# Score and row-maximum matmuls of the softmax heads, divided over four 32-column tiles

## The chip, the cores and the metric

One core of a Trainium2 chip runs the whole program in one launch. The metric is device time in microseconds. Three runs of the kernel before gave 8461.63, 8458.88 and 8468.84 us, median 8461.63.

## The reference

The input is 4 images of 48 x 48 tokens (N = 2304) with 192 channels, and the program is a chain of residual blocks on it: rotary attention, a Fourier mixer, wide attention, a switch of experts, retention with a decay mask, and a projection by signs. The change touches the first block alone. There every image has 8 heads of width 12, so 32 heads in all, and what is computed for a head is

```
attn = einsum('bhnd,bhmd->bhnm', q * hd ** -0.5, k)      # 2304 x 2304
attn = softmax(attn, axis=-1)
out  = einsum('bhnm,bhmd->bhnd', attn, v)                # 2304 x 12
```

## The kernel before

The attention of the first block is the function `softmax_heads`. An earlier stage has split q and k of every head into three bf16 terms each, whose sum is the fp32 value. Stacked along the contraction they give products of terms: 8 x 12 = 96 rows. So every score is one bf16 matmul with 96 rows, or 99 where three further rows carry the negated row maximum in three bf16 terms against ones.

For each head the stage does two things. The **row maximum** goes through TensorE once: for each of 18 tiles of 128 queries (stationary, `q_next`), `max_chunk` (L522 to L535) multiplies by 5 chunks of keys (moving, `k_next`): four of 512 columns and one of 256, 90 chunks a head. A chunk is written to one of two PSUM buffers, `ring`; VectorE reduces it to a column (L624) and frees it by the semaphore `ring_free`, for which TensorE waits at L533 before chunk m+2. At the head's end VectorE reduces the 90 columns (L628), TensorE transposes them (L540), and VectorE splits them into terms (L632 to L641), which go through DRAM into the rows of q.

Then come 54 **steps**, one for each third of the queries (768) and each tile of 128 keys. `score` (L542 to L556) has the 128 keys stationary (`k_piece`) and the queries moving in two halves of 384 columns, into one of two PSUM buffers `scores`. ScalarE takes the exponential of the 768 columns (L664) into one of four buffers `probs`. `value` (L558 to L568) multiplies them by the values, fp32: the stationary operand is `v_piece`, 32 columns wide (12 values, a column of ones, zeros), and the 768 queries are divided into four groups of 192 moving columns, each of which is written to its own quarter of PSUM's partitions, so to its own 32-column tile of the array. The profile shows an fp32 matmul as two instructions with a load each, eight in a step.

The order of TensorE's work is written out in `exponentials` (L570 to L602): in step n the scores of n, then chunks, the values of n - 2, then chunks. The chunks belong to the next head; of its 90 chunks 23 (`AHEAD`) are done a head before that, the others are spread evenly by the list in `maxima`. A head thus has 108 places for 90 chunks, five in each six. The steps of two heads are written out in one body of a hardware loop, which runs 15 times; heads 30 and 31 follow it, with 67 chunks in head 30 and none in head 31. Before the loop the 90 chunks of head 0 run alone.

SyncE loads q, k and v of the next head, GpSimd loads `q_next` and `k_next` and stores the results; both wait on the same semaphores (`scored`, `valued`, `ring_full`), which the last matmul of a piece of work raises.

Of the kernel before, what the change touches and what calls it, by code (L numbers as in the profile page):

```python
# [8 lines left out]
P = 128  # L9
# [360 lines left out]
def softmax_heads(nc, q_parts, k_parts, q_runs, k_runs, v_rows, ident, m_rows, out_rows, N, d, scale):  # L370
# [16 lines left out]
    QC = THIRD // 2  # L387
# [4 lines left out]
    PT = TILES // PIECES  # L392
# [8 lines left out]
    with ExitStack() as ctx:  # L401
        sb, ps, sem = allocators(nc, ctx, "softmax")
        q_third = [sb(f"q_third{i}", [K + 3, THIRD], BF16) for i in range(3)]
        k_piece = [sb(f"k_piece{i}", [K + 3, PT * P], BF16) for i in range(PIECES)]
        v_piece = [sb(f"v_piece{i}", [P, PT, 32], F32) for i in range(PIECES)]
        q_next = [sb(f"q_next{i}", [K, N], BF16) for i in range(2)]
        k_next = [sb(f"k_next{i}", [K, N], BF16) for i in range(2)]
# [8 lines left out]
        scores = [ps(f"scores{i}", [P, 2, 512], F32) for i in range(2)]  # L416
        sums = [ps(f"sums{i}", [P, 512], F32) for i in range(2)]
        ring = [ps(f"ring{i}", [P, 512], F32) for i in range(2)]
# [5 lines left out]
        ring_full, ring_free = sem("ring_full"), sem("ring_free")  # L424
# [98 lines left out]
        @block.tensor  # L523
        def _(pe):
            def max_chunk(h, i, m):

                j, c = divmod(m, NC)
                at, width = CHUNKS[c]
                if m == 0:

                    pe.wait_ge(next_in[i], (h - i + 2) * 16 * RUNS)

                pe.wait_ge(ring_free, h * RING + max(m - 1, 0))  # L533
                return nc.tensor.matmul(ring[m % 2][:, 0:width], q_next[i][:, j * P:(j + 1) * P],  # L534
                                        k_next[i][:, at:at + width], start=True, stop=True).then_inc(ring_full, 1)  # L535

            def max_transpose(h):
                pe.wait_ge(ring_free, h * RING + MAXES - 1)
                pe.wait_ge(row_ready, h + 1)
                nc.tensor.transpose(ring[MAXES % 2][0:TILES, 0:P], row_max[:, :], identity[:, :]).then_inc(ring_full, 1)  # L540

            def score(h, n, first=False):  # L542
                third, t = divmod(n, TILES)
                if t == 0:
                    pe.wait_ge(q_in[third], (h + 1) * 16 * RUNS)
                    pe.wait_ge(maxes_in[third], (h + 1) * 16)
                if third == 0 and t % PT == 0:
                    pe.wait_ge(kv_in[t // PT], (h + 1) * 16 * (RUNS + 1))

                if n or not first:  # L550
                    pe.wait_ge(exped, h * STEPS + n - 1)
                for c in range(2):
                    last = nc.tensor.matmul(scores[n % 2][:, c, 0:QC],  # L553
                                            k_piece[t // PT][:, t % PT * P:(t % PT + 1) * P],
                                            q_third[third][:, c * QC:(c + 1) * QC], start=True, stop=True)
                last.then_inc(scored, 1)  # L556

            def value(h, n):  # L558
                third, t = divmod(n, TILES)
                pe.wait_ge(exped, h * STEPS + n + 1)  # L560
                if t == 0:

                    pe.wait_ge(copied, h * 3 + max(third - 1, 0))
                for g in range(4):
                    last = nc.tensor.matmul(sums[third % 2][32 * g:32 * g + 32, 0:VC], v_piece[t // PT][:, t % PT, :],  # L565
                                            probs[n % 4][:, g * VC:(g + 1) * VC],
                                            start=(t == 0), stop=(t == TILES - 1))
                last.then_inc(valued, 1)  # L568

            def exponentials(h, i, following):  # L570

                done = 0

                def maxima(n):

                    nonlocal done
                    turn, steps = 2 * TURN, 2 * STEPS
                    share = AHEAD + (MAXES - AHEAD) * (n + 1) // turn if n < turn else MAXES + AHEAD * (n + 1 - turn) // (steps - turn)
                    while following and done < min(share, MAXES if following == 1 else MAXES + AHEAD):
                        if done == MAXES:  # L580
                            max_transpose(h + 1)
                        if done < MAXES:
                            max_chunk(h + 1, 1 - i, done)
                        else:
                            max_chunk(h + 2, i, done - MAXES)
                        done += 1
                    if following == 1 and done == MAXES and n == turn:
                        max_transpose(h + 1)

                done = AHEAD  # L590
                for n in range(STEPS):

                    if n:
                        score(h, n)
                    maxima(2 * n)
                    if n >= 2:
                        value(h, n - 2)
                    maxima(2 * n + 1)
                if following:
                    score(h + 1, 0)  # L600
                value(h, STEPS - 2)
                value(h, STEPS - 1)  # L602

            pe.wait_ge(ident_in, 16)
            pe.wait_ge(ones_set, PIECES)
            for m in range(MAXES):
                max_chunk(0, 0, m)
            max_transpose(0)
            for m in range(AHEAD):
                max_chunk(1, 1, m)  # L610
            score(0, 0, first=True)
            with pe.Fori(0, n_heads // 2 - 1) as pair:
                for i in range(2):
                    exponentials(pair * 2 + i, i, 2)
            exponentials(n_heads - 2, 0, 1)
            exponentials(n_heads - 1, 1, 0)
# [2319 lines left out]
```

## Time and profile before

| | |
|---|---|
| median of 3 runs | 8461.63 us |
| span of the profiled execution | 8460.6 us |
| TensorE busy, of the span | 7417.9 us (88%) |
| weight loads busy | 3625.5 us (43%) |
| VectorE busy | 4769.0 us (56%) |
| ScalarE busy | 3185.4 us (38%) |
| GpSimd busy | 2338.1 us (28%) |
| the stage `softmax_heads` | about 297 to 2630 us |
| mean granted TensorE clock | 0.915 |

The profiled execution has no time of its own beside its span, from its first to its last instruction. PE is TensorE's matmuls, PEld its weight loads, DVE is VectorE, ACT is ScalarE, SP is SyncE. The time of a matmul is from its start to its modelled end; since the next one starts as soon as the columns of this one have streamed in, the difference of two starts says what a matmul costs, and its duration how long its result takes.

### The profile page before, as it was taken

What the parts mean: (1) busy time and instruction counts of PE and PEld (TensorE: products, weight loads), DVE (VectorE), ACT (ScalarE), POOL (GpSimd) and SP (SyncE); (2) the same over time, 40 slices, a digit from 0 to 9 for tenths busy, and PEclk for the clock granted to TensorE, in tenths of its full rate; (3) what the DMA queues carried; (4) which work ended last, traced back from release to release, by engine and by line L of the source; (5) the groups of instructions that cost most, each with busy time, mean ns of one, the idle gap of its engine ahead of it and who ended that gap; (6) DMA issues with size and microseconds to landing.
All of it is one profiled execution on the core that took longest, in us unless ns stands there. A gap on an engine that the chain in (4) does not pass through costs nothing. (4 is left out here: it accounts for less than half of the span.)

```text
span 8460.6 us, 164061 instructions
## 1 busy us (share of the span) xinstructions
PE 7417.9 (88%) x53035; PEld 3625.5 (43%) x53035; DVE 4769.0 (56%) x7714; ACT 3185.4 (38%) x5336; POOL 2338.1 (28%) x2558
## 2 busy tenths in 40 slices
PE   6799999999996775799999970997799999999987
PEld 4233333333333552576666760775433333333326
DVE  6777777777772401232232243114677777777766
ACT  2166666666663241222222210212444444444432
POOL 0011111111111000000000003002388888888861
PEclk8699999999998786899999965998899999999986
DMA  4211111111114314000000031114611111111113
GB/s 118 58 33 33 33 33 33 33 33 33 33 29 95 104 46 132 27 13 13 26 1 17 1 119 54 52 49 135 200 31 30 30 31 29 30 30 31 30 50 105
DMA packets 414311, 426.01 MB, mean 50 GB/s; under 512 B 76199, under 2 KB 386635, under 8 KB 408590
## 3 DMA queue, kind: packets, MB, share of 16 engines
q1 hardware_dynamic: 331790, 339.52, 14.2%
q0 software_dynamic: 62400, 59.16, 2.8%
q10 hardware_dynamic: 19712, 21.53, 0.8%
q8 instruction: 299, 4.90, 0.3%
q14 instruction: 110, 0.90, 0.0%
HBM read 253.37 MB, written 166.55 MB: 50 GB/s over the span
## 5 line engine op out<-in xcount | busy, mean ns | idle before, releaser
L624 DVE TENSOR_REDUCE softmax_part_max<-softmax_ring 128x1 f32<-128x512 f32 (+1 forms) x2880 | 1727.2, 634 | 494.0 <-PE softmax_ring L534 464.0
L2421 DVE TENSOR_TENSOR retention_decayed<-retention_scores,retention_decay_table 128x768 f32<-128x768 f32 x1728 | 1655.4, 958 | 475.0 <-PE retention_scores L2381 475.0
L2440 POOL TENSOR_TENSOR retention_decayed<-retention_third,retention_decay_table 128x384 f32<-128x384 f32 x1728 | 1723.4, 997 | 456.7 <-ACT retention_third L2462 415.5
L664 ACT ACTIVATE softmax_probs<-softmax_scores 128x768 f32<-128x768 f32 x1728 | 1399.2, 811 | 885.8 <-PE softmax_scores L553 847.3
L2462 ACT COPY retention_third<-retention_scores 128x384 f32<-128x384 f32 x1728 | 827.9, 479 | 1276.6 <-PE retention_scores L2381 1276.6
L534 PE MATMUL softmax_ring<-softmax_k_next,softmax_q_next 96*128 96x512 bf16 (+1 forms) x2880 | 1086.5, 379 | 139.7 <-DVE softmax_part_max L624 49.7
L2394 PE MATMUL retention_sums<-retention_decayed,retention_v_piece 128*32 128x288 f32 x13824 | 1197.8, 418 | 0.5 <-POOL retention_decayed L2440 0.5
L2381 PE MATMUL retention_scores<-retention_q_half,retention_k_piece 96*128 96x384 bf16 x5184 | 1145.7, 330 | 29.4 <-DMA retention_v_piece<-ret_v 29.3
L565 PE MATMUL softmax_sums<-softmax_probs,softmax_v_piece 128*32 128x192 f32 x13824 | 930.2, 343 | 0.6 <-ACT softmax_result L653 0.5
L553 PE MATMUL softmax_scores<-softmax_q_third,softmax_k_piece 99*128 99x384 bf16 x3456 | 870.8, 333 | 5.9 <-ACT softmax_probs L664 5.9
L2381 PEld LDWEIGHTS retention_scores<-retention_q_half,retention_k_piece 96*128 96x128 bf16 x5184 | 366.6, 98 | 947.2 <-issue 832.2
L500 POOL DMA_DIRECT2D rope_out<-softmax_result x384 | 195.4, 510 | 1946.4 <-ACT softmax_result L653 1892.2
L1473 DVE TENSOR_REDUCE wide_top<-wide_scores 128x1 f32<-128x2304 f32 x72 | 184.2, 2558 | 753.1 <-PE wide_scores L1371 753.1
L534 PEld LDWEIGHTS softmax_ring<-softmax_k_next,softmax_q_next 96*128 96x128 bf16 x2880 | 279.6, 97 | 747.3 <-DVE softmax_part_max L624 397.9
L1371 PE MATMUL wide_scores<-wide_qk_t 96*128 96x512 f32 (+1 forms) x1440 | 568.9, 550 | 2.6 <-ACT wide_v L1445 2.6
L565 PEld LDWEIGHTS softmax_sums<-softmax_probs,softmax_v_piece 128*32 128x32 f32 x13824 | 277.4, 109 | 561.0 <-issue 408.4
L2394 PEld LDWEIGHTS retention_sums<-retention_decayed,retention_v_piece 128*32 128x32 f32 x13824 | 272.0, 108 | 549.6 <-DVE retention_decayed L2421 533.2
L1397 PE MATMUL wide_valued_bank<-wide_v,wide_probs_t 128*128 128x192 f32 x2592 | 433.5, 326 | 2.1 <-ACT wide_probs_t L1461 2.1
L553 PEld LDWEIGHTS softmax_scores<-softmax_q_third,softmax_k_piece 99*128 99x128 bf16 x3456 | 314.4, 99 | 266.5 <-issue 109.0
L1397 PEld LDWEIGHTS wide_valued_bank<-wide_v,wide_probs_t 128*128 128x128 f32 x2592 | 424.9, 190 | 6.6 <-DVE wide_probs_t L1483 3.1
L1452 ACT ACTIVATE wide_probs<-wide_scores,wide_shift 128x2304 f32<-128x2304 f32 x72 | 157.1, 2182 | 693.1 <-DVE wide_shift L1475 693.1
L1371 PEld LDWEIGHTS wide_scores<-wide_qk_t 96*128 96x128 f32 x1440 | 267.8, 190 | 283.2 <-issue 279.4
(299 smaller groups left out, 6483.4 us busy)
## 6 DMA issues: line engine op xcount, KB each, us to landing
ret_v<-ret_proj_values SPq DMA_DIRECT2D x8, 1728.0 KB, 8.8
retention_v_piece<-ret_v SPq DMA_DIRECT2D x144, 96.0 KB
softmax_q_third<-rope_q SPq DMA_DIRECT2D x192, 54.0 KB
softmax_q_next<-rope_q POOLq DMA_DIRECT2D x64, 162.0 KB, 3.9
softmax_k_piece<-rope_k SPq DMA_DIRECT2D x192, 54.0 KB
softmax_k_next<-rope_k POOLq DMA_DIRECT2D x64, 162.0 KB, 5.5
ret_q<-ret_proj_parts SPq DMA_DIRECT2D x48, 216.0 KB
ret_k<-ret_proj_parts SPq DMA_DIRECT2D x48, 216.0 KB
```

Source lines behind the costliest of these rows:

```text
L534: return nc.tensor.matmul(ring[m % 2][:, 0:width], q_next[i][:, j * P:(j + 1) * P], k_next[i][:, at:at + width], start=True, stop=True).th ...
L553: last = nc.tensor.matmul(scores[n % 2][:, c, 0:QC], k_piece[t // PT][:, t % PT * P:(t % PT + 1) * P], q_third[third][:, c * QC:(c + 1) * ...
L565: last = nc.tensor.matmul(sums[third % 2][32 * g:32 * g + 32, 0:VC], v_piece[t // PT][:, t % PT, :], probs[n % 4][:, g * VC:(g + 1) * VC], ...
L624: nc.vector.reduce_max(part_max[:, j, c:c + 1], ring[m % 2][:, 0:CHUNKS[c][1]], axis=X)\
L664: nc.scalar.activation(probs[n % 4][:, :].rearrange("p (c q) -> p c q", c=2), scores[n % 2][:, :, 0:QC], ACT.Exp, scale=scale).then_inc(ex ...
L1371: last = nc.tensor.matmul(scores[:, at:at + width], qk_t[:, 0, f, i * P:(i + 1) * P], qk_t[:, 1, f, at:at + width], start=(f == 0), stop=( ...
L1397: last = nc.tensor.matmul(valued_bank[:, 0:C], probs_t[:, t * P:(t + 1) * P], v[:, t, :], start=(t == 0), stop=(t == TILES - 1))
L2381: last = nc.tensor.matmul(scores[n % 2][:, c, 0:QC], k_piece[t // PT][:, t % PT * P:(t % PT + 1) * P], q_half[half][:, c * QC:(c + 1) * QC ...
L2394: last = nc.tensor.matmul(sums[half][32 * g:32 * g + 32, 0:VC], v_piece[t // PT][:, t % PT, :], weights[n % 4][:, g * VC:(g + 1) * VC], st ...
L2421: nc.vector.tensor_tensor(weights[n % 4][:, 0:2 * QC].rearrange("p (c q) -> p c q", c=2), scores[n % 2][:, 0:2, 0:QC], table[:, table_at(n ...
L2440: nc.gpsimd.tensor_tensor(weights[n % 4][:, 2 * QC:HALF], third[n % 3][:, :], table[:, at:at + QC], ALU.mult)\
L2462: nc.scalar.copy(third[n % 3][:, :], scores[n % 2][:, 2, 0:QC]).then_inc(third_copied, 1)
```

## The change

Each matmul of a chunk and each half of a score is divided into four. Matmul g has 32 of the 128 stationary columns and writes 32 of the 128 PSUM partitions, so it stands on column tile g, as value matmul g does. All four stream the same moving columns. The semaphores are raised by the last of the four; the waits are where they were.

```diff
@@ max_chunk
                 pe.wait_ge(ring_free, h * RING + max(m - 1, 0))
-                return nc.tensor.matmul(ring[m % 2][:, 0:width], q_next[i][:, j * P:(j + 1) * P],
-                                        k_next[i][:, at:at + width], start=True, stop=True).then_inc(ring_full, 1)
+                for g in range(4):
+                    rows = j * P + 32 * g
+                    last = nc.tensor.matmul(ring[m % 2][32 * g:32 * g + 32, 0:width], q_next[i][:, rows:rows + 32],
+                                            k_next[i][:, at:at + width], start=True, stop=True)
+                last.then_inc(ring_full, 1)
@@ score
                 for c in range(2):
-                    last = nc.tensor.matmul(scores[n % 2][:, c, 0:QC],
-                                            k_piece[t // PT][:, t % PT * P:(t % PT + 1) * P],
-                                            q_third[third][:, c * QC:(c + 1) * QC], start=True, stop=True)
+                    for g in range(4):
+                        at = t % PT * P + 32 * g
+                        last = nc.tensor.matmul(scores[n % 2][32 * g:32 * g + 32, c, 0:QC], k_piece[t // PT][:, at:at + 32],
+                                                q_third[third][:, c * QC:(c + 1) * QC], start=True, stop=True)
                 last.then_inc(scored, 1)
```

## Rows read from the trace of the kernel before

**Rows 1.** The page: span, busy time by engine, the span in 40 slices.
```profile
span 8460.6 us, 164061 instructions
PE 7417.9 (88%) x53035; PEld 3625.5 (43%) x53035; DVE 4769.0 (56%) x7714; ACT 3185.4 (38%) x5336; POOL 2338.1 (28%) x2558
...
PE   6799999999996775799999970997799999999987
...
PEclk8699999999998786899999965998899999999986
```
**Rows 2.** The page's groups: busy us, mean ns | idle before, releaser.
```profile
L624 DVE TENSOR_REDUCE softmax_part_max<-softmax_ring 128x1 f32<-128x512 f32 (+1 forms) x2880 | 1727.2, 634 | 494.0 <-PE softmax_ring L534 464.0
...
L664 ACT ACTIVATE softmax_probs<-softmax_scores 128x768 f32<-128x768 f32 x1728 | 1399.2, 811 | 885.8 <-PE softmax_scores L553 847.3
...
L534 PE MATMUL softmax_ring<-softmax_k_next,softmax_q_next 96*128 96x512 bf16 (+1 forms) x2880 | 1086.5, 379 | 139.7 <-DVE softmax_part_max L624 49.7
...
L565 PE MATMUL softmax_sums<-softmax_probs,softmax_v_piece 128*32 128x192 f32 x13824 | 930.2, 343 | 0.6 <-ACT softmax_result L653 0.5
L553 PE MATMUL softmax_scores<-softmax_q_third,softmax_k_piece 99*128 99x384 bf16 x3456 | 870.8, 333 | 5.9 <-ACT softmax_probs L664 5.9
```
**Rows 3.** Windows: stretch, length, busy by engine, clock, DMA share, GB/s.
```profile
495.20:569.20 74.00, 69.29 (x639) 24.53 (x631) 55.60 (x96) 44.41 (x58) 9.44 (x19) 0.95 0.12 32
...
427.20:495.20 68.00, 66.36 (x639) 23.96 (x631) 55.41 (x97) 44.34 (x58) 9.98 (x19) 1.00 0.14 34
2567.10:2630.00 62.90, 61.24 (x689) 18.75 (x687) 1.97 (x8) 55.40 (x71) 7.97 (x16) 1.00 0.07 19
297.00:358.60 61.60, 47.41 (x90) 9.28 (x90) 52.65 (x91) 0.00 (x0) 0.46 (x1) 0.50 0.04 14
```
**Rows 4.** Waits, 443 to 511 us: total us, times, longest.
```profile
ACT softmax_probs L664 <- PE softmax_scores L553: 22.7, 52, 1.4
...
DVE softmax_part_max L624 <- PE softmax_ring L534: 10.9, 34, 0.8
PEld softmax_ring L534 <- DVE softmax_part_max L624: 10.4, 30, 1.2
```
**Rows 5.** Timeline, 1012.3 to 1016.3 us: start, length, engine, line, count.
```profile
1012.18 0.49 PE L553 MATMUL softmax_scores<-softmax_q_third,softmax_k_piece 99*128 99x384 bf16 x2
1012.60 0.16 PEld L565 LDWEIGHTS softmax_sums<-softmax_probs,softmax_v_piece 128*32 128x32 f32 x8 [0.32 <-issue]
1012.60 0.53 PE L565 MATMUL softmax_sums<-softmax_probs,softmax_v_piece 128*32 128x192 f32 x8
...
1013.06 0.39 PE L534 MATMUL softmax_ring<-softmax_k_next,softmax_q_next 96*128 96x512 bf16 x1
...
1013.29 0.49 PE L553 MATMUL softmax_scores<-softmax_q_third,softmax_k_piece 99*128 99x384 bf16 x2
...
1013.49 1.02 DVE L624 TENSOR_REDUCE softmax_part_max<-softmax_ring 128x1 f32<-128x512 f32 x2 [0.42 <-PE softmax_ring L534]
1013.62 0.27 PE L534 MATMUL softmax_ring<-softmax_k_next,softmax_q_next 96*128 96x256 bf16 x1
...
1013.82 0.53 PE L565 MATMUL softmax_sums<-softmax_probs,softmax_v_piece 128*32 128x192 f32 x8
...
1016.26 0.37 PE L565 MATMUL softmax_sums<-softmax_probs,softmax_v_piece 128*32 128x192 f32 x4
```
**Rows 6.** Timeline, two value blocks back to back, 943.1 to 944.5 us.
```profile
943.58 0.48 PEld L565 LDWEIGHTS softmax_sums<-softmax_probs,softmax_v_piece 128*32 128x32 f32 x16 [0.32 <-issue]
943.58 0.86 PE L565 MATMUL softmax_sums<-softmax_probs,softmax_v_piece 128*32 128x192 f32 x16
```
**Rows 7.** DMA queues, 375 to 2570 us: packets, MB, share of 16 engines.
```profile
q8 instruction: 197, 3.23, 0.6%
```
**Rows 8.** Waits around the loop's branch, 511 to 527 us.
```profile
PEld softmax_ring L534 <- issue: 3.8, 3, 3.5
```
**Rows 9.** Timeline of the first head's chunks, 310 to 314 us.
```profile
311.28 3.02 DVE L624 TENSOR_REDUCE softmax_part_max<-softmax_ring 128x1 f32<-128x512 f32 x5 [0.37 <-PE softmax_ring L534]
```

## The prediction

> **What bounds the kernel now.** I read the page first. The one core spans 8460.6 us with TensorE 88% busy, and the slices show TensorE at 9 and the clock at 9 from about 280 to 2630 us, which is the stage that the change touches [rows 1]. The chain of waits on the page covers about 1% of the span (the last stage), so it says nothing here. The groups of instructions name three engines in the stage [rows 2]: VectorE reduces 2880 row-maximum chunks (L624), ScalarE takes 1728 exponentials (L664), and TensorE feeds both (L534, L553) and multiplies by the values (L565). The table of windows then sizes a head. A head in the middle of the pair takes 68.0 us, with TensorE busy 66.4, VectorE 55.4 and ScalarE 44.3 at clock 1.00; a head that begins after the loop's branch takes 74.0 at clock 0.95 [rows 3]. So the stage costs about 71 us a head, 32 heads. In the waits of one such head ScalarE waits 22.7 us for scores and VectorE 10.9 us for the ring, both on TensorE, while TensorE's loads wait 10.4 us on VectorE [rows 4]: TensorE is the bound, VectorE comes next and is coupled to it through a ring of two buffers, ScalarE is last.
>
> **What TensorE does with a head.** The timeline shows one cycle of three steps, from the value block at 1012.60 to the one at 1016.26, 3.66 us [rows 5]; 54 steps are 18 cycles, 65.9 of the 68.0 us. In a cycle lie three score pairs (2 x 384 columns), five chunks (4 x 512 and 1 x 256, since 90 chunks fall on 54 steps) and three value blocks of eight matmuls. A score pair is 0.49 us long where one matmul is 0.33, so 384 bf16 columns stream in 0.16 us. The scores follow a 512-column chunk after 0.23 and a chunk follows a pair after 0.33 (1013.06, 1013.29, 1013.62): among matmuls 128 columns wide nothing is lost. The bf16 streams of a cycle are 4608 columns, 1.92 us. A value block is two rounds of four 192-column matmuls, one on each 32-column tile; eight take 0.53 and sixteen back to back 0.86 [rows 5, 6], so a round costs 0.165 us: four tiles stream at once, or it would be near 0.66. The six rounds of a cycle are 0.96 to 0.99. Sum of streams: 2.9 us. The other 0.76 us is mostly at the six places where a 128-column matmul and a 32-column one meet. Into a block: scores begin at 1012.18, their two streams end at 1012.50, values begin at 1012.60, 0.10 lost. Out of a block: 1012.60 to 1013.06 is 0.46 for 0.33 to 0.35 of rounds, 0.11 to 0.13 lost. The loads of a value block start with the block itself, after the pause [rows 5]. Three steps lose 0.63 to 0.69 us, 11.3 to 12.4 us a head; what is left, about 0.1, is waits.
>
> **What the change removes.** With everything on 32-column tiles the six pauses of a cycle should go. I take all of 0.65. Nothing of the trace shows a bf16 to fp32 change on one tile shape, so the lower bound of this term is zero (first rival).
>
> The Trainium skill, TensorEngine Tiling, Key Properties, says that changing the tiling mode, and not merely the tile, drains the engine. The pauses agree with it as to place and say 0.1 us each; by it the whole term goes.
>
> **What it adds.** Each bf16 matmul becomes four with a load each: 16 instead of 4 instructions a score, 8 instead of 2 a chunk. Streams: if a quad streams at once, as the value rounds do, a chunk stays 0.21 us and a score 2 x 0.16. The nearest row is the fp32 round: 0.165 for what is 0.160 of stream [rows 6]. So 11 quads a cycle at 0.005 more are 0.06 us; the other end is a quad that streams one after the other, four times 1.92 (third rival). I take 0.06, because the four tiles already read four moving operands at once. Loads: sixteen loads of a pair of blocks lie inside 0.48 us while the matmuls run [rows 6], eight begin with a block and take 0.16 [rows 5]; hidden, cost 0, and if the cover fails it is the fourth rival. The last tile of a quad starts some 0.02 us after the first (four loads and matmuls enter in that time, by the 0.16 us of eight loads of 0.11 each), so scores and chunks are complete 0.02 later.
>
> The Trainium skill, TensorEngine Tiling, Restrictions, says that column tiling disables fast weight load. The 128-column bf16 loads may then be the faster kind now, but the load of a 32-column tile is hidden here either way, by the value blocks.
>
> Program: TensorE's loop over two heads grows from about 2520 to 4900 matrix instructions. The instruction queue brings 197 blocks in 2195 us, one per 11 us, 3.23 MB or 16.4 KB each [rows 7]; that becomes one per 5.5 us. At the branch, where nothing is ahead, TensorE misses 3.5 us [rows 8]; this is below 5.5, so with one block ahead the supply holds. Cost 0; the branch stays once per pair. If supply were late by 1 us per block it would be 11 us a head.
>
> **What is late next.** Once the pauses are gone TensorE would need 2.88 + 0.06 + some 0.04 = 2.98 us a cycle. The ring then decides. A buffer's round is matmul 0.39, 0.04 to VectorE (1013.06 to 1013.49), reduction 0.69, and about 0.05 back to TensorE, 1.18, now 1.20. Between chunk m and m+2 TensorE has chunk, values, chunk, scores: 0.21 + 0.33 + 0.21 + 0.33 = 1.08. It waits 0.12 for each such pair of chunks; a cycle has two, less what the 256-column chunk (reduction 0.41) and the one empty slot give: I take 0.20 in all. VectorE alone needs 5 reductions in 3.02 us with its last one's tail, about 2.8 a cycle [rows 9], below. ScalarE needs 3 x 0.81 = 2.4, below. So a cycle goes from 3.66 to 3.18 + about 0.02 = 3.20, saving 0.46, 8.3 us a head (to 59.7, with VectorE busy 55.4 unchanged). The end of a head (row maxima, transpose, terms) is a chain through VectorE, unchanged. Bounds: VectorE's own 55.4 plus nothing, a gain of 12.6 a head; and zero.
>
> **Sum.** Thirty heads with all maxima: 30 x 8.3 = 249. Head 30 has 40 steps with maxima: 13.3 x 0.46 = 6. The last 71 exponentials without maxima take 62.9 us with ScalarE busy 55.4 [rows 3]; TensorE would need less than that, so ScalarE bounds them at about 58: 5. The first head's 90 chunks, alone at clock 0.50 in 61.6 us [rows 3], gain no pause and pay 0.01 to 0.02 each: +1. Other stages run the same instructions. 8460.6 - 249 - 6 - 5 + 1 = 8201.6. The profiled execution's span stands 1.0 us below the median of the runs, 8461.6, so 8203.
>
> **Rivals.** (1) *The pause belongs to the change between bf16 and fp32, not to the tile shape.* For: at every pause both change together [rows 5]. Against: nothing in a 32-column matmul's rows asks for it, and the change of row count (96 to 99) is free. Price: the pauses stay, completion is 0.02 later, 8455 to 8485. Chance 0.07.
> (2) *A quad has a price of its own*, 0.03 to 0.05 us each (the first round of a block alone is some 0.02 longer than the later ones: 0.53 for two rounds against 0.86 for four). Eleven quads are 0.33 to 0.55, of which the 0.20 of ring waits hides a part. The gain falls to 0.1 to 0.3 a cycle: 8290 to 8400. Chance 0.10.
> (3) *Four bf16 streams do not run at once* (slower). Place: every quad; the fp32 rounds take 0.83 ns a column where bf16 takes 0.42, so the tiles have been seen to run at once only at half the bf16 pace. If two streams share, the 1.92 us of a cycle becomes 3.84, a cycle 2.98 + 1.92 = 4.9, +1.2 x 18 x 31 = +690: 9150. It decides from a factor of about 1.35 on the bf16 streams, where 0.65 of pauses is eaten. Chance 0.05.
> (4) *Loads no longer hide* (slower). The Trainium skill, TensorE: Matmul & The Clock Gate, Part 3, says that a load overlaps running matmuls only when the row group differs. Worked from rows: all quads here use the same rows, so each of the 11 would show its load of about 0.1 us, 1.1 against 0.65: +0.45 x 18 x 31 = +250, 8710. Against it stand the sixteen loads within the running value matmuls [rows 6]. Chance 0.03, and 0.02 for a program supply that falls behind, with a similar price.
>
> **Numbers.** About 0.2% (17 us) is what the measurement can tell. The forecast has 0.73, its own range 8130 to 8270: it spans savings of 6 to 10.5 us a head, by how much the ring gives back. With rival (2) the range 8130 to 8350 holds about 0.8. Faster: 0.73 + 0.10 = 0.83. Same: 0.06, most of (1). Slower: 0.11, the rest.
>
> **What would show it.** In an undisturbed head: about 60 us instead of 68.0. Value blocks should begin 0.33 after a score pair begins, and a chunk 0.33 to 0.35 after a value block begins, instead of 0.42 and 0.46. Chunk to scores 0.22: rival (3) if 0.4 or more, (2) if 0.25. The loads' waits on VectorE at L534 should grow from 10.4 us a head, VectorE's on TensorE fall below 6, ScalarE's 22.7 fall to about 15. If the 0.1 us pause is still there beside the value blocks, (1) holds. I am wrong if a head takes more than 63 us or less than 57.

## The result and the profile after

The changed kernel takes 8254.3 us (median of 4 runs, 8240.9 to 8257.8) against 8461.7 for the kernel before: ratio 0.975, 95% interval 0.974 to 0.977, a gain of 207 us where 259 were forecast. Its profiled execution spans 8256.2 us and took 8257.8.

The page after, as in [rows 1] and [rows 2]. TensorE has 19,008 matmuls more and is busy 258 us less.

```profile
span 8256.2 us, 202077 instructions
...
PE 7159.8 (87%) x72043; PEld 3924.8 (48%) x72043; DVE 4722.4 (57%) x7714; ACT 3174.3 (38%) x5336; POOL 2340.3 (28%) x2558
...
L628 DVE TENSOR_REDUCE softmax_part_max<-softmax_ring 128x1 f32<-128x512 f32 (+1 forms) x2880 | 1680.6, 633 | 329.2 <-PE softmax_ring L536 272.1
...
L668 ACT ACTIVATE softmax_probs<-softmax_scores 128x768 f32<-128x768 f32 x1728 | 1392.4, 810 | 675.0 <-PE softmax_scores L558 602.3
...
L536 PE MATMUL softmax_ring<-softmax_k_next,softmax_q_next 96*32 96x512 bf16 (+1 forms) x11520 | 1119.5, 378 | 177.1 <-issue 68.2
```

VectorE's idle time before its reductions fell from 494.0 to 329.2 us and ScalarE's before its exponentials from 885.8 to 675.0. Four times as many chunk matmuls are busy for almost the same time (1086.5 before, 1119.5 now): the four run at once.

The timeline of the kernel after, as in [rows 5] (start, length, engine, line, count). By the prediction's readings of the rows before, the columns of a piece of work stream in 0.21 us for a 512-column chunk, 0.11 for a 256-column chunk, 0.32 for a step's scores and 0.33 for a step's values; what the distance of two starts has beyond that is a pause or a wait.

```profile
1011.68 0.28 PE L536 MATMUL softmax_ring<-softmax_k_next,softmax_q_next 96*32 96x256 bf16 x4
1011.68 0.23 PEld L569 LDWEIGHTS softmax_sums<-softmax_probs,softmax_v_piece 128*32 128x32 f32 x8
1011.79 0.50 PE L569 MATMUL softmax_sums<-softmax_probs,softmax_v_piece 128*32 128x192 f32 x8
1012.32 0.10 PEld L536 LDWEIGHTS softmax_ring<-softmax_k_next,softmax_q_next 96*32 96x32 bf16 x4 [0.41 <-DVE softmax_part_max L628]
1012.32 0.40 PE L536 MATMUL softmax_ring<-softmax_k_next,softmax_q_next 96*32 96x512 bf16 x4
1012.41 0.25 PEld L558 LDWEIGHTS softmax_scores<-softmax_q_third,softmax_k_piece 99*32 99x32 bf16 x8
1012.55 0.50 PE L558 MATMUL softmax_scores<-softmax_q_third,softmax_k_piece 99*32 99x384 bf16 x8
...
1012.88 0.39 PE L536 MATMUL softmax_ring<-softmax_k_next,softmax_q_next 96*32 96x512 bf16 x4
1012.88 0.34 PEld L569 LDWEIGHTS softmax_sums<-softmax_probs,softmax_v_piece 128*32 128x32 f32 x8
1013.10 0.50 PE L569 MATMUL softmax_sums<-softmax_probs,softmax_v_piece 128*32 128x192 f32 x8
...
1014.08 0.50 PE L569 MATMUL softmax_sums<-softmax_probs,softmax_v_piece 128*32 128x192 f32 x8
1014.25 0.10 PEld L536 LDWEIGHTS softmax_ring<-softmax_k_next,softmax_q_next 96*32 96x32 bf16 x4
1014.30 0.81 ACT L668 ACTIVATE softmax_probs<-softmax_scores 128x768 f32<-128x768 f32 x1 [0.39 <-PE softmax_scores L558]
1014.41 0.39 PE L536 MATMUL softmax_ring<-softmax_k_next,softmax_q_next 96*32 96x512 bf16 x4
```

The chunk of 512 columns at 1012.88 is followed by the values at 1013.10, 0.22 later; the values at 1014.08 by a chunk at 1014.41, 0.33 later; the loads of the values start at 1012.88, while the chunk still streams. No pause is left between bf16 and fp32. What stands in its place is the wait at 1012.32: the values began at 1011.79 and were streamed in by 1012.12 (0.33 later), and the chunk waited 0.2 us more for VectorE to free its buffer.

Windows (length, busy by engine, clock) of an undisturbed head and of one after the branch, as in [rows 3], and the waits of an undisturbed one, as in [rows 4]:

```profile
424.10:484.90 60.80, 58.34 (x1229) 33.38 (x1229) 53.94 (x96) 44.17 (x57) 9.70 (x19) 1.00 0.16 40
484.90:552.60 67.70, 61.44 (x1225) 33.56 (x1225) 54.23 (x96) 44.35 (x57) 9.46 (x18) 0.92 0.14 36
```

```profile
ACT softmax_probs L668 <- PE softmax_scores L558: 15.3, 35, 1.4
PEld softmax_ring L536 <- DVE softmax_part_max L628: 12.5, 36, 1.3
DVE softmax_part_max L628 <- PE softmax_ring L536: 4.3, 18, 0.7
```

From the first exponential of one head to that of the next, an undisturbed head takes 60.3 us instead of 68.0, and a pair of heads, which holds one branch of TensorE's loop, 129.5 on the mean instead of 143.1. Only every fourth head is undisturbed: ScalarE has a loop of its own with four heads in its body, and its branch stands beside every second one of TensorE's. The waits for nothing that the profile shows ("issue"), before TensorE's matmuls over the whole stage, are these in the kernel after and then in the kernel before (total us, times, longest):

```profile
PE softmax_ring L536 <- issue: 68.2, 24, 4.6
...
PE softmax_sums L569 <- issue: 11.0, 12, 1.7
```

```profile
PE softmax_ring L534 <- issue: 44.0, 14, 3.4
```

That is 35 us more, in 36 places, more than the loop has rounds (15). The timeline behind one branch of the kernel after shows such a place:

```profile
892.30 0.62 PE L536 MATMUL softmax_ring<-softmax_k_next,softmax_q_next 96*32 96x512 bf16 x4 [3.05 <-issue]
...
893.34 0.43 PE L536 MATMUL softmax_ring<-softmax_k_next,softmax_q_next 96*32 96x256 bf16 x4
895.20 0.62 PE L536 MATMUL softmax_ring<-softmax_k_next,softmax_q_next 96*32 96x512 bf16 x4 [1.43 <-DVE softmax_part_max L628]
```

```profile
892.97 0.69 DVE L628 TENSOR_REDUCE softmax_part_max<-softmax_ring 128x1 f32<-128x512 f32 x1 [4.13 <-PE softmax_ring L536]
893.82 0.42 DVE L628 TENSOR_REDUCE softmax_part_max<-softmax_ring 128x1 f32<-128x256 f32 x1 [0.16 <-PE softmax_ring L536]
```

The profile puts the stop of 1.43 us down to VectorE. But the chunk at 895.20 needs the buffer of the chunk at 892.30, whose reduction ended at 893.66, and even the later reduction ended at 894.24, almost one us before TensorE went on. It is the second stop of the branch: the next block of code came late. Code comes by a DMA queue of its own, in blocks of 16.4 KB; only TensorE's code has changed, and the kernel after takes 350 blocks in 2040 us where the one before took 197 in 2195 (packets, MB, share):

```profile
q8 instruction: 350, 5.73, 1.2%
```

In that queue's records one block is fetched from 889.82 to 890.78 us, and TensorE goes on at 892.30; the next from 892.88 to 893.98, and TensorE goes on at 895.20. All 14 branches between 500 and 2200 us have this second stop, 1.4 to 2.8 us long and 28 us together; the first stops are 46 us together (2.7 to 4.6 each), about as before (44.0). Eight further stops (0.7 to 1.7 us, 10 together) stand in the middle of the loop's body, before the values. Each of these stops (14, 14 and 8) ends 1.2 to 2.3 us after the end of a block's fetch. In the kernel before no second stop for code follows a branch.

Every run below has runs of the kernel before beside it on the same chip (medians 8458 to 8465 us), and its ratio is to those; 8461 us stands for it in differences.

### The profile page after: what moved, and what is told of

It reads as the page before. It is cut to its first block and busy times, and to the rows that moved or that the text cites. A ratio compares the mean times of both kernels' runs of the same rounds, so it can differ in the third digit from the quotient of the medians.

```text
span 8256.2 us, 202077 instructions
## 1 busy us (share of the span) xinstructions
PE 7159.8 (87%) x72043; PEld 3924.8 (48%) x72043; DVE 4722.4 (57%) x7714; ACT 3174.3 (38%) x5336; POOL 2340.3 (28%) x2558
## 5 line engine op out<-in xcount | busy, mean ns | idle before, releaser
L628 DVE TENSOR_REDUCE softmax_part_max<-softmax_ring 128x1 f32<-128x512 f32 (+1 forms) x2880 | 1680.6, 633 | 329.2 <-PE softmax_ring L536 272.1
L668 ACT ACTIVATE softmax_probs<-softmax_scores 128x768 f32<-128x768 f32 x1728 | 1392.4, 810 | 675.0 <-PE softmax_scores L558 602.3
L536 PE MATMUL softmax_ring<-softmax_k_next,softmax_q_next 96*32 96x512 bf16 (+1 forms) x11520 | 1119.5, 378 | 177.1 <-issue 68.2
L569 PE MATMUL softmax_sums<-softmax_probs,softmax_v_piece 128*32 128x192 f32 x13824 | 885.9, 330 | 11.7 <-issue 11.0
L558 PE MATMUL softmax_scores<-softmax_q_third,softmax_k_piece 99*32 99x384 bf16 x13824 | 889.6, 332 | 2.9 <-DMA softmax_v_piece<-rope_v 1.8
L536 PEld LDWEIGHTS softmax_ring<-softmax_k_next,softmax_q_next 96*32 96x32 bf16 x11520 | 308.2, 95 | 675.8 <-DVE softmax_part_max L628 444.3
L569 PEld LDWEIGHTS softmax_sums<-softmax_probs,softmax_v_piece 128*32 128x32 f32 x13824 | 427.4, 112 | 206.6 <-issue 26.8
L558 PEld LDWEIGHTS softmax_scores<-softmax_q_third,softmax_k_piece 99*32 99x32 bf16 x13824 | 364.8, 97 | 178.7 <-ACT softmax_probs L668 24.9
```

What stands on the lines that cost most here:

```text
L536: last = nc.tensor.matmul(ring[m % 2][32 * g:32 * g + 32, 0:width], q_next[i][:, rows:rows + 32], k_next[i][:, at:at + width], start=True, ...
L558: last = nc.tensor.matmul(scores[n % 2][32 * g:32 * g + 32, c, 0:QC], k_piece[t // PT][:, at:at + 32], q_third[third][:, c * QC:(c + 1) * ...
L628: nc.vector.reduce_max(part_max[:, j, c:c + 1], ring[m % 2][:, 0:CHUNKS[c][1]], axis=X)\
L668: nc.scalar.activation(probs[n % 4][:, :].rearrange("p (c q) -> p c q", c=2), scores[n % 2][:, :, 0:QC], ACT.Exp, scale=scale).then_inc(ex ...
```

## The experiments

**Where the pause belongs.** Three kernels divide one part alone, or divide into wider tiles.

```diff
 # scores alone: max_chunk as in the kernel before
-                for g in range(4):  ... ring[m % 2][32 * g:32 * g + 32, 0:width]
+                nc.tensor.matmul(ring[m % 2][:, 0:width], q_next[i][:, j * P:(j + 1) * P], ...
```

> Only the score matmuls stand on four 32-column tiles; the row-maximum chunks are 128 columns wide again. Theory (about 0.1 us at every place where the tile shape changes): a chunk now lies between two pieces of 32-column work, so a cycle of three steps has 10 changes of shape where the kernel before had 6; 4 x 0.1 more is 3.66 + 0.4 = 4.06 us a cycle, 7 us more a head than before, about 8680 us. Rival (the pause belonged to the change between bf16 and fp32): as many type changes as in the changed kernel, which has no pause, so about 8254. In the trace 0.09 to 0.10 us on each side of every chunk, also between a bf16 chunk and bf16 scores, which only the theory expects.

Measured: 8758 us, ratio 1.035 (1.031 to 1.038). The timeline:

```profile
465.86 0.39 PE L534 MATMUL softmax_ring<-softmax_k_next,softmax_q_next 96*128 96x512 bf16 x1
466.18 0.51 PE L555 MATMUL softmax_scores<-softmax_q_third,softmax_k_piece 99*32 99x384 bf16 x8
466.62 0.28 PE L534 MATMUL softmax_ring<-softmax_k_next,softmax_q_next 96*128 96x256 bf16 x1
```

From a 512-column chunk (0.21 of stream) to scores 0.32, from scores (0.32) to a chunk 0.44: 0.1 us both ways, and both are bf16. So the change of the tile's shape costs, not that of the type. An undisturbed head takes 75.0 us, the 7 more that were expected. The total is 78 us above the forecast of 8680. At least a part of that goes with the clock: it is at half for 266 us of the stage, in the kernel before for 133. After eight of the branches it stays there for 14 to 51 us, where in the kernel before it is back after 7 to 10 (once 17), as in this window (length, PE, PEld, DVE, ACT, POOL, clock, DMA share, GB/s):

```profile
1160.00:1259.00 99.00, 94.77 (x959) 27.64 (x955) 58.57 (x97) 44.51 (x57) 9.57 (x18) 0.74 0.09 24
```

```diff
 # chunks alone: score as in the kernel before
-                    for g in range(4):  ... scores[n % 2][32 * g:32 * g + 32, c, 0:QC]
+                    nc.tensor.matmul(scores[n % 2][:, c, 0:QC], k_piece[t // PT][:, t % PT * P:(t % PT + 1) * P], ...
```

> Only the row-maximum chunks stand on 32-column tiles; scores are 128 columns wide. Theory (shape): the scores are the only wide work, so each step has one change into them and one out of them, 6 a cycle as before: about 8460, with the pauses moved from the value blocks to the scores. Rival (type): 8254. A second rival, that quads have a price of their own that the changed kernel hides under ring waits: 8460 plus 5 chunks x 18 x 31 x that price, 8515 at 0.02 us.

Measured: 8470.9 us, ratio 1.001 (1.000 to 1.002), no gain. The pauses have moved to the scores: from a chunk to scores 0.32 for 0.21 of stream, from scores to values 0.43 for 0.32. From values to a chunk it is 0.35 for 0.33, without a pause:

```profile
1012.03 0.39 PE L536 MATMUL softmax_ring<-softmax_k_next,softmax_q_next 96*32 96x512 bf16 x4
1012.35 0.50 PE L556 MATMUL softmax_scores<-softmax_q_third,softmax_k_piece 99*128 99x384 bf16 x2
1012.78 0.53 PE L568 MATMUL softmax_sums<-softmax_probs,softmax_v_piece 128*32 128x192 f32 x8
1013.13 0.40 PE L536 MATMUL softmax_ring<-softmax_k_next,softmax_q_next 96*32 96x512 bf16 x4
```

```diff
 # pairs on 64-column tiles, in max_chunk and score
-                for g in range(4):
-                    rows = j * P + 32 * g
+                for g in range(2):
+                    rows = j * P + 64 * g
```

> Scores and chunks as pairs on 64-column tiles, values on 32-column tiles as before. Theory (any change of tile shape drains): the same 6 changes a cycle as in the kernel before, about 8460 us, pauses of 0.1 us at the value blocks. Rival (only the undivided array has to drain, tiles of different width overlap): about 8254.

Measured: 8491.2 us, ratio 1.004 (1.002 to 1.005). Tiles of 64 beside tiles of 32 pay like undivided ones: scores at 1011.67, the chunk at 1012.02, then 0.21 for 0.11 of stream:

```profile
1012.02 0.28 PE L536 MATMUL softmax_ring<-softmax_k_next,softmax_q_next 96*64 96x256 bf16 x2
1012.23 0.53 PE L569 MATMUL softmax_sums<-softmax_probs,softmax_v_piece 128*32 128x192 f32 x8
```

What the Trainium skill, TensorEngine Tiling, Key Properties, says of a drain when the tiling mode changes agrees with all three runs, at 0.1 us a change.

**In what order tiles take their matmuls.**

```diff
-                for c in range(2):
-                    for g in range(4):
+                for g in range(4):
+                    for c in range(2):
```

> As the changed kernel, but a score's eight matmuls go tile by tile (both halves of the queries on tile 0, then on tile 1, ...), not half by half. Theory (matmuls start in order, and two run at once only if they are on different tiles): the second half on a tile starts 0.16 us after the first, so a score lasts 5 x 0.16 = 0.80 instead of 0.32 us; +0.48 x 54 = 26 us of TensorE work a head, partly in place of ring waits, about 21 a head, 8900 us. Rival (the queue lets a matmul on a free tile go ahead): 8254.

Measured: 8237.8 us (two runs, 8234.8 and 8240.8), ratio 0.973 (0.971 to 0.975), as the changed kernel. My theory was wrong. The eight matmuls together are as short as before, though each tile's two stand one behind the other in the program:

```profile
1011.82 0.50 PE L558 MATMUL softmax_scores<-softmax_q_third,softmax_k_piece 99*32 99x384 bf16 x8
1012.19 0.40 PE L536 MATMUL softmax_ring<-softmax_k_next,softmax_q_next 96*32 96x512 bf16 x4
```

A matmul for a free tile goes ahead of one that waits for its tile. The changed kernel's own trace shows it too, behind one of its stops: the program has eight matmuls of the values ahead of the chunk's four, and two of the chunk's start before the last of the values'.

```profile
951.76 0.36 PE L569 MATMUL softmax_sums<-softmax_probs,softmax_v_piece 128*32 128x192 f32 x3 [1.55 <-issue]
951.87 0.46 PE L536 MATMUL softmax_ring<-softmax_k_next,softmax_q_next 96*32 96x512 bf16 x2
951.95 0.33 PE L569 MATMUL softmax_sums<-softmax_probs,softmax_v_piece 128*32 128x192 f32 x2
```

The Trainium skill, TensorE: Matmul & The Clock Gate, Part 3, says that matmuls are strictly in order in start and end; by the 0.37 us between the two rows of the tile-by-tile kernel, where strict order would need 0.80 by my estimate, that doesn't hold across column tiles.

**Where the missing gain went: the branch and the supply of code.** In the first kernel TensorE's loop has four heads in its body, in the second none is looped; the third is the kernel before without the loop.

```diff
-            with pe.Fori(0, n_heads // 2 - 1) as pair:
-                for i in range(2):
-                    exponentials(pair * 2 + i, i, 2)
+            with pe.Fori(0, n_heads // 4 - 1) as four:
+                for i in range(4):
+                    exponentials(four * 4 + i, i % 2, 2)
+            for i in range(2):
+                exponentials(n_heads - 4 + i, i, 2)
 # without a branch: "for pair in range(n_heads // 2 - 1):" in the loop's place
```

> The changed kernel with four heads in TensorE's loop body (7 rounds, then 4 heads written out) instead of two (15 rounds, then 2): 7 branches instead of 15. Theory A (each branch costs the 3.5 us without instructions, a second gap of 1.4 to 2.6 us three us later when the second block of code is late, and the half clock after it, some 8 us in all; supply in a straight run is good): 8 branches fewer, 8254 - 8 x 8 = 8190. Theory B (supply is short all along, the gaps come per block and not per branch): the branch alone goes, 8 x 3.5 = 28, 8226. No-effect rival (the gaps are hidden behind ScalarE's own branch every four heads): within 10 of 8254.

Measured: 8189.1 us, ratio 0.968 (0.966 to 0.969).

> The changed kernel with all heads of TensorE written out, no branch. Theory A: 15 branches fewer, 8254 - 15 x 8 = 8134, half-clock stretches gone from the stage except at ScalarE's branches, heads of 60 to 61 us throughout. Theory B: 8254 - 15 x 3.5 = 8200, with gaps of 1.5 us still every few blocks. Against e5 it says whether the gain goes with the number of branches (a factor of 15/8).

Measured: 8175.6 us, ratio 0.967 (0.965 to 0.969).

> The kernel before with all heads of TensorE written out. It says what a branch costs where code is used up half as fast: pairs take 143.1 us there against 2 x 68.0, so 7.1 a branch; 15 of them 106, so 8355. If the changed kernel's branch costs more (8.9 by 129.5 against 2 x 60.3), the difference of the two gains, some 27 us, is what code supply took of the predicted gain, and straight against straight gives about 8355 - 8125 = 230. Rival (code supply took nothing): both kernels gain the same from it and straight against straight is 207.

Measured: 8423.7 us, ratio 0.995 (0.993 to 0.997).

Eight branches fewer save 65 us, fifteen 79: theory A met the first and missed the second by 41 us. It had put the whole of the disturbed heads down to TensorE. Without its branch every fourth head still takes 65 to 67 us, at ScalarE's branch. Where TensorE had branched alone the head falls by 7.9 us (68.5 to 60.6 on the mean), where both engines had branched in one place the two heads fall by 0.8 together. The kernel before gains only 37 us for 15 branches (expected 106), the changed one 79. The difference, 42 us, is near the 35 us of additional "issue" waits above. By ratios (0.9751 - 0.9667 and 1 - 0.9951), each from runs of one chip, it is 30 us, with some 20 of uncertainty. Without branches the two kernels lie 248 us apart instead of 207. In the changed kernel without TensorE's branch the waits for code before its matmuls are nearly gone (total us, times, longest; 380 to 2400 us):

```profile
PE softmax_ring L536 <- issue: 2.2, 2, 1.2
```

The half clock does not explain the difference: it lasts 133 us of the stage before and 126 after, and 71 in both kernels without TensorE's branch.

ScalarE's branch, taken away from the second kernel:

```diff
-            with act.Fori(0, n_heads // GROUP) as group:
-                for i in range(GROUP):
-                    exponentials(group * GROUP + i, i == 0, i == GROUP - 1)
+            for h in range(n_heads):
+                exponentials(h, h == 0, h == n_heads - 1)
```

> TensorE and ScalarE both without a branch. In the run without TensorE's branch every fourth head still takes 65 to 67 us against 60.1, with a stretch of half clock, at the place of ScalarE's branch. Theory: these 7 places vanish, 7 x 6 = 42 less than 8176: about 8134, and no half-clock stretch between 400 and 2300 us. Rival (the stretches belong to something else that comes every four heads): 8176.

Measured: 8133.0 us, ratio 0.961 (0.958 to 0.963), as expected; between 500 and 2100 us the granted clock is 0.99, against 0.97 in the changed kernel, and no head takes more than 62.0 us.

**What bounds a cycle now.**

```diff
-                    nc.vector.reduce_max(part_max[:, j, c:c + 1], ring[m % 2][:, 0:CHUNKS[c][1]], axis=X)\
+                    nc.vector.reduce_max(part_max[:, j, c:c + 1], ring[m % 2][:, 0:CHUNKS[c][1] // 2], axis=X)\
```

> The changed kernel with VectorE reducing only the first half of each chunk's columns (it leaves out half of the row-maximum reduction, so the maxima are those of half the keys); TensorE's work is the same. A buffer's round falls from 1.20 to about 0.85 us. Theory (what holds the changed kernel is the ring's two buffers, 0.2 to 0.3 us a cycle): the cycle falls from about 3.2 to about 2.98, 4 to 5 us a head, 8254 - 31 x 4.5 = 8115, and the load's waits on VectorE at the chunks nearly vanish. Rival (TensorE's own work bounds it, quads cost more than I took): within 20 of 8254.

Measured: 8083.9 us, ratio 0.955 (0.953 to 0.957); an undisturbed head takes 55.6 us, 4.7 less. Of the 174 us between the two profiled executions 148 are the heads and 14 the first head's chunks. The waits of a stretch of 100 us (600 to 700) fall to this, from 18.5 in the branchless kernel:

```profile
PEld softmax_ring L536 <- DVE softmax_part_max L628: 1.5, 2, 1.0
```

Is it VectorE's time, or the time that a buffer needs for its round? The next kernel (no branch in TensorE) keeps VectorE's work and has three buffers:

```diff
-        sums = [ps(f"sums{i}", [P, 512], F32) for i in range(2)]
-        ring = [ps(f"ring{i}", [P, 512], F32) for i in range(2)]
+        sums = [ps("sums0", [P, 512], F32)] * 2
+        ring = [ps(f"ring{i}", [P, 512], F32) for i in range(3)]
@@ max_chunk, value; ring[m % 3] everywhere
-                pe.wait_ge(ring_free, h * RING + max(m - 1, 0))
+                pe.wait_ge(ring_free, h * RING + max(m - 2, 0))
-                    pe.wait_ge(copied, h * 3 + max(third - 1, 0))
+                    pe.wait_ge(copied, h * 3 + third)
```

> TensorE without the branch (8176 us so far), the ring with three buffers, the third one in the bank that the second buffer of the sums had; the values of a third therefore wait until ScalarE has copied the sums of the third before. Theory (ring waits are 4.7 us a head, as the half reduction showed): nearly all of it comes back, minus a wait of at most 0.6 us at each of three thirds: net 2.5 to 4.5 a head, 8040 to 8100. Rival (the half reduction gained by VectorE's time, not by the buffers' latency): no gain from a buffer, the thirds' waits alone, 8175 to 8230.

Measured: 8035.2 us, ratio 0.949 (0.947 to 0.952), 140 less than with two buffers; an undisturbed head takes 56.3 us, with VectorE busy 52.89:

```profile
477.20:533.80 56.60, 54.70 (x1231) 40.02 (x1227) 52.89 (x96) 44.11 (x58) 9.57 (x18) 1.00 0.17 42
```

So the round of two buffers was the bound: 3.8 us a head came back (60.1 to 56.3), of the 4.7 that the half reduction had shown, and the first head's chunks are 15 us shorter; 8035 lies 5 us below the range that I gave.

The last stop that I could name was at the end of a head (two buffers again, no branch in TensorE):

```diff
-                pe.wait_ge(ring_free, h * RING + max(m - 1, 0))
+                pe.wait_ge(ring_free, max(h * RING + m - 1, 0))
 # the buffer is (m + h) % 2; VectorE's loop, one head a round, now has two
-            with dve.Fori(0, n_heads) as h:
-                maxima(h)
+            with dve.Fori(0, n_heads // 2) as pair:
+                for i in range(2):
+                    maxima(pair * 2 + i, i)
```

> TensorE without the branch, and the two ring buffers taken in turns across heads (91 uses a head are odd, so the last transpose and the next head's first chunk now fall on different buffers and the chunk need not wait for the row maxima's copy). VectorE's loop has two heads in its body. Theory: the stop of about 0.9 us at each head's end goes, 31 x 0.9 = 28 less than 8176: about 8148. Rival (the chunk is only moved, VectorE takes it up after the same row of small instructions): 8176.

Measured: 8259.1 us, ratio 0.976 (0.974 to 0.979), 83 us more than the branchless kernel without it. Undisturbed heads fell from 60.1 to 59.8 only: the chunk was merely moved, as the rival had it. And VectorE's longer body brought a stop at each of its branches (440 to 1400 us, this kernel and then the one with one head a round):

```profile
DVE softmax_part_max L628 <- issue: 26.8, 7, 4.2
```

```profile
DVE softmax_part_max L628 <- issue: 3.1, 15, 0.2
```

One head's reductions in the body cost at most 0.2 us at a branch, two heads' nearly 4: 15 x 3.8 = 57 of the 83 us, if each costs its full length. The rest may be the half clock, 146 us of the stage instead of 71; no run separates the two.

**Together**: three buffers, and neither TensorE nor ScalarE with a branch.

> Three ring buffers, one buffer of sums, TensorE and ScalarE both without a branch; VectorE's loop stays one head long. Theory (the two gains stand in different places, the ring's wait in every cycle, ScalarE's branch in every fourth head): they add, 8035 - 42 = 7993. Rival (the branch's stop was partly made good by the wait it fell into): 8010 to 8035.

Measured: 7987.2 us (median of 5 runs), ratio 0.944 (0.942 to 0.946), the fastest kernel here, 6 us below the forecast. From 500 to 2100 us VectorE is busy 94% (third number), TensorE 97%, at clock 1.00:

```profile
500.00:2100.00 1600.00, 1544.10 (x34678) 1180.51 (x34673) 1499.86 (x2719) 1248.74 (x1614) 265.74 (x501) 1.00 0.16 41
```

## Why the prediction was right, and by what it was too good

The mechanism held; the gain was forecast 52 us too large.

- **The six pauses of a cycle**, 0.65 us, all taken as gone: right. They are absent in the trace after; the scores-only and chunks-only runs show 0.1 us wherever the shape changes, and the type costs nothing (rival 1).
- **Quads at 0.005 us, loads hidden**: right. 0.22 from a 512-column chunk to the next work, 0.16 between the halves of a score; the last matmul of a quad starts 0.01 us after the first, not 0.02. Rivals 2 to 4 fell. Against rival 4, with what the Trainium skill, TensorE: Matmul & The Clock Gate, Part 3, says of loads and row groups, stands 1012.88: the loads of the values start with the chunk's matmuls, on the same rows. Of the fast weight load, which column tiling disables by the Trainium skill, TensorEngine Tiling, Restrictions, no price shows: a bf16 load of 32 columns takes 0.09 to 0.10 us, as one of 128 columns did, and is hidden.
- **The ring's waits**, 0.20 a cycle or 3.6 us a head: undersized. Halving the reduction took 4.7 us off a head, and the head without them is then 55.6 us, where my other terms add up to 56.1. I had 59.7 us a head and measured 60.3, so 0.6 x 30 = 18 us of the gain are missing here. The waits on VectorE that were to grow from 10.4 a head are 12.5; VectorE's on TensorE fell to 4.3 and ScalarE's to 15.3, as forecast; VectorE's busy time, which I had unchanged at 55.4, is 53.9.
- **"with one block ahead the supply holds. Cost 0"**: this is the step that failed. 350 blocks of code in 2040 us are one in 5.8, near the 5.5 that I had forecast, and without a branch the supply does hold (2.2 us of waits). Behind a branch it does not. I had compared the time of one block with the 3.5 us of the stop as if a block were always ahead; the second block is fetched from 892.88 us on, when TensorE had gone on with the first at 892.30, and after 32 loads and matmuls TensorE stood from 893.8 to 895.2. How far this comes from TensorE using a block in half the time, and how far from where in a block the branch lands, no run separates. In the body's middle the supply fails too, in eight places. The price: the 30 heads of the loop take 103 us more than 30 undisturbed ones before and 127 after, so 24 us; the branchless pair says 42 (30 by ratios). The additional stops add up to more (35 by the "issue" waits, 40 with the four second stops that the profile puts down to VectorE): a part of them falls into waits that were there anyway.
- **Heads 30 and 31**, 11 us: 110.0 us before and 96.8 after (to the start of the last exponential), 13.
- The sum: of the stage's 260 us, 18 + 24 - 2 = 40 are missing, and 219.5 were measured. The first exponential comes 1.5 us later, where I had 1. What follows the stage took 5831 us before and 5845 after. It is the same code in every kernel here, and took 5820 to 5849 us in the other twelve profiled executions, so these 14 us are scatter.

So the right order of size is not luck. The mechanism was measured part by part, and no large errors cancel.

## What to carry to other kernels

Count how often a matmul stream changes the shape of its tiles: each change costs about 0.1 us here, into the other shape and out of it, and dividing wide matmuls into quads on the small tiles removes it at no price in streams. Divide all of them or none; one part alone moves the pauses (chunks only) or adds to them (scores only, 10 a cycle instead of 6). Multiplying the instructions of an engine raises its need for code, which showed here first behind the branch of a loop, where the block after the first came late. Look then for the next thing in line, which here was a ring of two buffers and was worth 140 us.

## What had not been expected of the hardware

- Column tiles of TensorE take their matmuls independently: program order among tiles does not delay a free one (0.37 us where order would need 0.80, by estimate).
- A loop body of VectorE with one head's 90 reductions branches in 0.2 us, with two heads' in almost 4.
- Behind a branch of TensorE's loop a second block of code can come late: 14 second stops of 1.4 to 2.8 us in the changed kernel, none in the kernel before.
- In the scores-only kernel, with 10 pauses a cycle, the granted clock stayed at the lower level (1.2 GHz) for 14 to 51 us behind eight of the stops at a branch. In the kernel before, with 6, it was back at 2.4 GHz after 7 to 10, once 17. What decides it no run shows.
